# The candidate's product with U5 stands two blocks into the next round's big product instead of four

## What is computed

```
h = relu(layernorm(x));  x = x + adj @ (h @ W0) + b0
h = relu(layernorm(x))
five times:
    m  = adj @ h ;  av = [m, m] ;  u = h @ U3^T + c3
    z  = sigmoid(av @ W3^T + b3 + u) ;  r = sigmoid(av @ W4^T + b4 + u)
    hv = tanh(av @ W5^T + b5 + (r * h) @ U5^T + c5)
    h  = (1 - z) * h + z * hv
x = x + h
```

## Time and profile before

| | |
|---|---|
| median of three runs | 1581.13 us |
| the profiled execution | 1581.27 us |
| its span, first to last instruction | 1579.4 us |
| mean granted TensorE clock | 0.994 of full speed |
| TensorE matmul busy | 1550.6 us, 98% |
| VectorE busy | 983.8 us, 62% |
| ScalarE busy | 701.2 us, 44% |
| GpSimd busy | 347.2 us, 22% |
| calls of `rh_lo` (L1087) and of U5's first matmul (L581) | 160 each, two to a candidate |

### The profile page before, as it was taken

One profiled execution on the slowest core, in us unless ns is written; L12 is line 12 of the kernel. 1 busy time (PEld: TensorE's weight loads), 2 busy tenths in 40 slices (PEclk: granted clock), 3 DMA queues, 4 the chain that ended last, 5 costly groups with the idle time before them and its releaser, 6 DMA issues.

```text
span 1579.4 us, 23033 instructions
## 1 busy us (share of the span) xinstructions
PE 1550.6 (98%) x7471; PEld 720.8 (46%) x7471; DVE 983.8 (62%) x1823; ACT 701.2 (44%) x1090; POOL 347.2 (22%) x817
## 2 busy tenths in 40 slices
PE   6899999999999999999999999999999999999997
PEld 4444444444444444444444444444444444444443
DVE  7675558655576556765567556675556755576556
ACT  3244434444444444444434444354443444344444
POOL 6230042300613006130062101530024300330000
PEclk8999999999999999999999999999999999999999
DMA  4121113211131111311113111221112211122111
GB/s 150 40 46 35 27 28 84 51 27 34 21 99 34 33 33 26 94 33 34 27 47 78 35 27 27 66 66 27 33 33 53 66 33 33 27 52 48 34 27 54
DMA packets 214238, 71.87 MB, mean 46 GB/s; under 512 B 208192, under 2 KB 209088, under 8 KB 214208
## 3 DMA queue, kind: packets, MB, share of 16 engines
q1 hardware_dynamic: 212480, 70.83, 19.4%
q10 hardware_dynamic: 1728, 0.66, 0.2%
HBM read 13.24 MB, written 8.39 MB: 14 GB/s over the span
## 4 chain that ended last, share of the span: by engine, by line
PE 95%; DVE 2%; DMA 1%; SPq 0%; issue 0%; ACT 0%; POOL 0%; DVEq 0%; POOLq 0%; ACTq 0%
PE ps_m L559 62%; PE ps_u L581 6%; PE ps_u L585 6%; PE ps_u L583 6%; PE ps_v L581 4%; PE ps_v L585 4%; PE ps_v L583 4%; DVE adj_lo L872 1%; DMA adj_in<-in_adj_dram 1%; PE ps_x L604 0%; PE ps_x L606 0%; PE ps_x L605 0%; POOL x_in L455 0%; SPq L393 0%; DMA h_lo<-nh_lo 0%
## 5 line engine op out<-in xcount | busy, mean ns | idle before, releaser
L559 PE MATMUL ps_m<-adj_hi,nh_hi 128*128 128x512 f16 x1280 | 485.1, 379 | 2.6 <-ACT nh_hi L732 2.6
L559 PE MATMUL ps_m<-adj_lo,nh_hi 128*128 128x512 f16 x1280 | 485.1, 379 | 0.0
L559 PE MATMUL ps_m<-adj_hi,nh_lo 128*128 128x512 f16 x1280 | 485.1, 379 | 0.0
L756 ACT ACTIVATE m_hi<-ps_m 128x512 f16<-128x512 f32 x192 | 113.2, 590 | 341.3 <-PE ps_m L559 341.3
L969 DVE SCALAR_TENSOR_TENSOR m_lo<-ps_m,m_hi 128x512 f16<-128x512 f32 x192 | 131.9, 687 | 203.6 <-ACT m_hi L756 203.3
L978 DVE SCALAR_TENSOR_TENSOR cand<-cand,h 128x512 f32<-128x512 f32 x160 | 107.9, 691 | 186.2 <-ACT cand L762 186.2
L309 POOL TENSOR_TENSOR mean<-stats 128x8 f32<-128x8 f32 x23 | 7.4, 322 | 871.7 <-DVE stats L908 871.7
L559 PEld LDWEIGHTS ps_m<-adj_hi,nh_lo 128*128 128x128 f16 x1280 | 125.3, 98 | 151.0
L559 PEld LDWEIGHTS ps_m<-adj_hi,nh_hi 128*128 128x128 f16 x1280 | 125.3, 98 | 150.6 <-issue 3.3
L559 PEld LDWEIGHTS ps_m<-adj_lo,nh_hi 128*128 128x128 f16 x1280 | 125.3, 98 | 147.2
L751 ACT ACTIVATE h_hi<-h 128x512 f16<-128x512 f32 x158 | 97.4, 630 | 209.3 <-DVE h L990 209.3
(11 more groups left out here) (136 smaller groups left out, 2050.2 us busy)
## 6 DMA issues: line engine op xcount, KB each, us to landing
x_in<-in_x_dram SPq DMA_DIRECT2D x16, 512.0 KB, 3.4
out_dram<-y SPq DMA_DIRECT2D x16, 512.0 KB, 2.7
adj_in<-in_adj_dram SPq DMA_DIRECT2D x8, 512.0 KB, 7.4
nh_hi<-h_hi SPq DMA_TRANSPOSE x128, 2.4
nh_lo<-h_lo SPq DMA_TRANSPOSE x128, 2.4
h_hi<-nh_hi SPq DMA_TRANSPOSE x32, 2.4
h_lo<-nh_lo SPq DMA_TRANSPOSE x32, 2.5
n_hi<-h_hi SPq DMA_TRANSPOSE x30, 2.4
```

The source lines that it names most:

```text
L559: last = nc.tensor.matmul(ps_m[half][:, :], a[slot][:, k, :], b[:, k, cols(half)], start=(k == 0 and n == 0), stop=(k == BLOCKS - 1 and n ...
L756: nc.scalar.activation(m_hi[:, cols(half)], ps_m[half][:, :], ACT.Copy, scale=M_SCALE).then_inc(m_hi_done, 1)
```

## The change

`finish_candidate` is issued behind 2 blocks of the first half instead of 4, in the steps and in the layer rounds. It and its waits are the same, and so is every other instruction; the blocks 2 and 3 (six matmuls) now follow it.

```diff
                 else:
-                    big_layer(p, slot, 0, range(HB))
+                    big_layer(p, slot, 0, range(AHEAD))
                     finish_candidate(n_step(p - 1, END, slot))
-                    big_layer(p, slot, 0, range(HB, BLOCKS))
+                    big_layer(p, slot, 0, range(AHEAD, BLOCKS))
                     big_layer(p, slot, 1, range(BLOCKS))
 
             def step(p, t, slot):
                 g, q, before = g_step(p, t, slot), n_step(p, t, slot), layer_before(p, t, slot)
                 if before is None:
-                    big_step(p, t, slot, 0, range(HB))
+                    big_step(p, t, slot, 0, range(AHEAD))
                     finish_candidate(q - 1)
-                    big_step(p, t, slot, 0, range(HB, BLOCKS))
+                    big_step(p, t, slot, 0, range(AHEAD, BLOCKS))
```

## The result

The changed kernel takes 1613.49 us (median of four runs, 1610.94 to 1614.40) against 1581.12 before. The ratio is 1.0202, with a 95% interval of 1.0184 to 1.0220: slower by 32.4 us. Its profiled execution is the fastest of the four: 1610.94 us, with a span of 1609.1, which is 29.7 more than the 1579.4 of the earlier trace rows.

The account below looks back on a forecast made before the run. TensorE, without waits between start and end, was taken to bound the kernel. 21 x 1.10 + 1.29 + 7 x 1.10 = 32.1 us on the profiled 1581.27, with the median 0.14 lower, gave 1613.2 us; range 1604.5 to 1618.

Parts of the forecast that it names:

- TensorE has no wait to lose: Between start and end TensorE waits for nothing, so moving work on it gains nothing and any new wait is paid in full.
- 50 ordinary rounds: nothing: In the 50 ordinary rounds blocks 0 and 1 cover rh_lo with 1.29 us to spare, so they cost nothing.
- 14 layer rounds, 1.10 each: Behind steps (END, 0) and (END, 1) of seven pairs, L726 and L944 delay rh_lo: U5 1.10 us late each.
- Behind step (0, 0), 7 x 1.10 and 1.29: Rounds behind step (0, 0): L732 and L951 make U5 1.10 us late in pairs 1 to 7; pair 0 loses 1.29 us.
- 7 bias add rounds, 1.10 each: Behind step (1, 0), GpSimd's bias add slows rh_lo's second half, so U5's second half loses 1.10 us in each of seven rounds.
- VectorE's block keeps its length, so I keep 1.10: Behind step (1, 0): VectorE's block lies within GpSimd's chain before and after, so the cost stays 1.10 us a round.
- the bias add out of the way at 0: Rival: the seven rounds behind step (1, 0) cost nothing, total 1605.5 us; chance 0.10.
- ahead of both halves: Rival: behind step (1, 0) the bias add starts before all of rh_lo, seven times 0.5 us more, 1616.7 us; chance 0.08.
- the case that I had kept: Behind step (1, 0) the bias add slows only rh_lo's second half as before the change, 1.10 us a round.
- The restart, 0.15 us: From the end of rh_lo to the U5 matmul that waits for it: 0.15 us, with 0.05 to either side.
- The clock: Rival: each new wait lets TensorE's clock drop, 70 us on top of the forecast, 1683 us; chance 0.03.

Follow-up runs that it names:

- slot 0's steps: Changed kernel with U5 behind two blocks only in the 32 steps of slot 0, four blocks elsewhere: 1581.13 us, ratio 0.9998.
- six blocks: Against the kernel before, U5 issued behind six blocks instead of four: 1580.24 us, ratio 0.9995.
- the steps alone: Changed kernel with U5 behind two blocks only in the 65 steps, layer rounds back at four: 1596.36 us, ratio 1.0097.

## Why the prediction was right, and which terms were off

The time was forecast as 1613.2 us and is 1613.49. Point by point:

- *TensorE has no wait to lose.* Right. Neither slot 0's steps nor six blocks gained anything that can be measured, and the candidate that comes 1.29 us earlier is worth nothing.
- *50 ordinary rounds: nothing.* Right, by the 32 moved alone and by their timelines.
- *14 layer rounds, 1.10 each.* Exact behind step (END, 0). Behind step (END, 1) the term was mis-sized: 1.29. I let the one stand for the other, though the earlier trace rows were from the first only. TensorE's wait one round earlier holds up VectorE and ScalarE but not GpSimd's normalisation (L455), so L944 meets another of its operations: L455 first starts 2.35 us ahead of the round instead of 1.33, and the second half of L944 takes 0.85 us instead of 0.68. With the bias add in eight pieces or later, when GpSimd is elsewhere in its work, these rounds lose 1.19 and 1.15 us. It is worth 1.3 us in all.
- *Behind step (0, 0), 7 x 1.10 and 1.29.* Exact, and 1.2 in pair 0, where U5's own lateness varies from run to run (0.93 to 1.08 us in the three profiles that keep four blocks there).
- *7 bias add rounds, 1.10 each.* The mechanism was right and the size wrong: 4.2 us in one profile and 5.7 in the other, instead of 7.7. The step that failed is "VectorE's block keeps its length, so I keep 1.10". The block keeps its length, but 1.29 us earlier it meets other operations of GpSimd's chain, L314 at its very start, and the bias add starts 1.15 us ahead of the round or 0.22 us behind its begin instead of 0.24 us ahead. Both rivals that I had priced happened, one in some rounds and one in others: the bias add out of the way at 0, and ahead of both halves; the case that I had kept happened in pair 0 of the first profile alone. The price of the latter rival was too high, 1.55 against 0.81: I put the bias add's start just ahead of `rh_lo` and it was 0.35 us ahead, `rh_lo` itself came 0.23 us sooner in the round, and its first half ended 0.55 us behind the bias add instead of 0.69.
- *The restart, 0.15 us.* Right: 1.10 came out to the hundredth in the rounds that GpSimd doesn't touch.
- *The clock.* No fall after any wait from 80 us on, nor with waits of 2 us. The argument for it was thinner than it looked: the row that I gave, 72 to 76 us, ends inside the wait that it was to speak for (from 76.3 to 81 us the clock was 1.00 too), and the kernel before also waits 2.6 us at 54 us and 1.5 us at 69 us. Up to 81 us the clock did fall in other profiles (last section). The swing of which the Trainium skill tells (TensorE: Matmul & The Clock Gate, A second HAM failure mode) did not come from 80 us on, where the short waits stand 29.6 us or more apart.

That the median was met to 0.3 us is partly luck: the bias add's term was 2 to 3.5 us too high, the layer term 1.3 too low, and the runs themselves spread over 3.5 us. The profiled execution, from which the terms are read, lost 29.8 us where the sum has 32.1.

## What to carry to other kernels

Where one engine runs without a wait, an instruction moved forward on it can only lose, and what it loses is the lateness of its latest input in each kind of round; read that lateness round kind by round kind, since a chain that is early in the common round may have other work queued inside it in a few. Ask the same of engines that aren't held up by the new wait: their work slides against the rest, and two long operations that shut each other out may change their order; where two operations start in the same instant, executions of one program can differ by it. The lost cover can be had back at the other end, by moving the work out of the chain into idle time of its engine.

## What the runs showed of the hardware

In three of the experiments the clock fell once where I had thought it safe, in the round behind step (0, 0) of pair 0. In the kernel with the bias add in eight pieces TensorE waited 1.5 us at 69 us and 2.2 us at 74 to 76 us, and the matmuls from 77.07 to 79.63 us then stood 0.43 us apart instead of 0.215. Stretches of that kernel (the column before the last two is the granted clock; 0.50 is 1.2 GHz):

```profile
72.00:76.00 4.00, 2.20 (x11) 0.75 (x8) 2.88 (x5) 1.72 (x3) 0.88 (x2) 1.00 0.44 89
76.00:78.00 2.00, 1.59 (x5) 0.66 (x6) 0.86 (x2) 1.73 (x4) 0.00 (x0) 0.65 0.42 85
78.00:80.00 2.00, 2.00 (x6) 0.68 (x5) 0.86 (x2) 1.29 (x2) 0.00 (x0) 0.50 0.00 0
80.00:84.00 4.00, 4.00 (x20) 1.84 (x19) 3.90 (x7) 1.64 (x3) 0.00 (x0) 1.00 0.01 4
```

It cost some 1.7 us (eight matmuls at 0.21 us more), once. The kernels with L726 and L944 moved and with the bias add later showed the same. The one with the steps alone had waits of 1.7 and 2.2 us in the same place and kept its full clock:

```profile
76.00:78.00 2.00, 1.47 (x7) 0.68 (x8) 0.99 (x2) 2.00 (x4) 0.00 (x0) 1.00 0.50 102
78.00:80.00 2.00, 2.00 (x11) 0.89 (x10) 1.70 (x3) 0.94 (x2) 0.00 (x0) 1.00 0.00 0
```

The clock also fell earlier, ahead of every moved product, in six of the thirteen profiles, both of the changed kernel among them. All thirteen have the wait of 2.6 us that ends at 54 us. The stretch behind it, in the kernel before and then in the changed kernel:

```profile
54.00:60.00 6.00, 5.87 (x46) 3.42 (x46) 1.39 (x2) 0.11 (x1) 0.00 (x0) 1.00 0.61 87
...
54.00:60.00 6.00, 5.87 (x29) 3.20 (x30) 1.38 (x2) 0.11 (x1) 0.00 (x0) 0.72 0.62 90
```

In the first profile of the changed kernel this cost nothing: the wait of 1.5 us at 69 us is gone there, and pair 0's late round begins at 72.67 us against 72.70 before. No profile with this earlier fall has the later one. What decides between them, in either place, was not tried and stays open.
